# Cross attention laid out by hand over its groups, its scales on GpSimd, and the combine product behind the up products

## The reference

```python
x = x + tanh(g_xattn[0]) * L0_xattn(layernorm(x), ctx, ctx, Wq, bq, Wk, bk, Wv, bv, Wo, bo)
#   16 heads of 8; head h sees keys h, h+16, h+32, h+48 (4 of them); softmax; out @ Wo.T + bo
x = x + tanh(g_ffn[0]) * L0_ffn(layernorm(x), ...)
#   rmsnorm, self attention of 16 heads over 128 tokens, residual, rmsnorm,
#   8 experts of 256 (2 chosen a token) and a shared one, residual
x = x + tanh(g_xattn[1]) * L1_xattn(ctx, layernorm(x), w_sim, b_sim, W_qv, b_qv)
x = x + tanh(g_ffn[1]) * L1_ffn(layernorm(x), ...)
#   16 experts of 64 (2 chosen), a gated shared one
return x
```

## Time and profile before

| | us |
|---|---|
| three runs | 563.38 median (563.04 to 566.1) |
| profiled execution | 563.62, its span 561.9 |
| mean granted TensorE clock | 0.929 of 2.4 GHz |
| busy: PE, DVE, ScalarE, GpSimd | 467.4, 403.4, 265.8, 257.3 |
| start and cross attention | 0 to 67 |
| self attention | 67 to about 190 |
| router | about 190 to 218 |
| mixtures | 218 to 562 |

### The profile page before, as it was taken

One profiled execution on the slowest core, in us unless ns is written; L12 is line 12 of the kernel. 1 busy time (PEld: TensorE's weight loads), 2 busy tenths in 40 slices (PEclk: granted clock), 3 DMA queues, 4 the chain that ended last, 5 costly groups with the idle time before them and its releaser, 6 DMA issues.

```text
span 561.9 us, 10894 instructions
## 1 busy us (share of the span) xinstructions
PE 467.4 (83%) x3679; PEld 349.4 (62%) x3679; DVE 403.4 (72%) x1051; ACT 265.8 (47%) x494; POOL 257.3 (46%) x363
## 2 busy tenths in 40 slices
PE   2576279999999466999979988999798989798896
PEld 2344147676667354777757776768576766576674
DVE  6567568888987644895775677777877787677763
ACT  0211057777776234655536533644355346443452
POOL 6000079988960030555554544345445444343453
PEclk9878589999999855999989997999899999998999
DMA  6500000201010000200000000000000000000000
GB/s 163 173 0 0 0 3 2 85 23 51 3 34 19 1 0 0 48 0 1 1 2 0 2 1 2 1 0 0 0 0 1 0 1 1 20 0 21 0 20 19
DMA packets 19325, 9.79 MB, mean 17 GB/s; under 512 B 6508, under 2 KB 18765, under 8 KB 19277
## 3 DMA queue, kind: packets, MB, share of 16 engines
q1 hardware_dynamic: 16829, 8.77, 5.5%
q10 hardware_dynamic: 2448, 0.40, 0.4%
HBM read 8.12 MB, written 1.05 MB: 16 GB/s over the span
## 4 chain that ended last, share of the span: by engine, by line
PE 60%; DVE 18%; issue 8%; POOL 5%; ACT 5%; ACTq 2%; DVEq 1%; POOLq 0%
PE PS L1453 11%; PE PS L1455 10%; PE PS L1454 10%; DVE work L1062 3%; PE PS L1334 3%; PE PS L1323 3%; PE PS L1498 3%; PE PS L1328 2%; PE PS L1368 2%; PE PS L1301 2%; PE PS L1417 2%; PE PS L1239 1%; PE PS L1312 1%; DVE t_b L736 1%; POOL W0L_gate L421 1%
## 5 line engine op out<-in xcount | busy, mean ns | idle before, releaser
L461 POOL TENSOR_TENSOR HLO<-work,HHI 128x512 fp32r<-128x512 f32 x112 | 145.1, 1296 | 185.9 <-ACT HHI L625 185.4
L632 ACT ACTIVATE work<-PS 128x512 f32<-128x512 f32 x112 | 66.8, 597 | 110.1 <-PE PS L1455 106.3
L1062 DVE TENSOR_TENSOR work<-work,PS 128x512 f32<-128x512 f32 x104 | 71.0, 683 | 55.1 <-ACT work L632 53.5
L625 ACT ACTIVATE HHI<-work 128x512 fp32r<-128x512 f32 x111 | 69.5, 626 | 40.2 <-DVE work L1067 40.1
L1067 DVE TENSOR_TENSOR work<-PS,work 128x512 f32<-128x512 f32 x112 | 77.1, 691 | 12.1 <-PE PS L1455 3.4
L1498 PE MATMUL PS<-CWT,sel 128*128 128x512 bf16 (+1 forms) x68 | 27.2, 400 | 24.0 <-DVE work L1062 24.0
L870 DVE TENSOR_REDUCE nmax<-PS 128x4 f32<-128x512 f32 x64 | 42.2, 682 | 6.4 <-PE PS L1301 6.2
L531 ACT ACTIVATE EX<-PS 128x512 f32<-128x512 f32 x64 | 35.2, 605 | 13.3 <-PE PS L1312 13.2
L1453 PE MATMUL PS<-H2H,W0H_up 128*128 128x512 f32 (+1 forms) x72 | 36.8, 512 | 2.9 <-DVE work L1067 2.9
L1453 PE MATMUL PS<-H2H,W0H_gate 128*128 128x512 f32 (+1 forms) x72 | 32.7, 454 | 2.2 <-issue 1.5
L1498 PEld LDWEIGHTS PS<-CWT,sel 128*128 128x128 bf16 x68 | 6.6, 97 | 44.8 <-DVE work L1062 30.0
(11 more groups left out here) (290 smaller groups left out, 1174.7 us busy)
## 6 DMA issues: line engine op xcount, KB each, us to landing
X<-in_x_dram SPq DMA_DIRECT2D x4, 256.0 KB, 8.1
raw<-in_L_ffn_e_gate_dram SPq DMA_DIRECT2D x1, 1024.0 KB, 5.4
raw<-in_L_ffn_e_up_dram SPq DMA_DIRECT2D x1, 1024.0 KB, 7.7
out_dram<-X SPq DMA_DIRECT2D x4, 256.0 KB, 2.3
ctx_nat<-in_ctx_dram SPq DMA_DIRECT2D x1, 616.0 KB
raw<-in_L_ffn_We_gate_dram SPq DMA_DIRECT2D x1, 512.0 KB, 4.0
raw<-in_L_ffn_We_up_dram SPq DMA_DIRECT2D x1, 512.0 KB, 3.9
raw<-in_L_ffn_We_down_dram SPq DMA_DIRECT2D x1, 512.0 KB, 4.1
```

Source lines behind the costliest of these rows:

```text
L461: pool.tensor_tensor(HLO[t][:], HH[k % 2][:], HHI[t][:].bitcast(F32), ALU.subtract).then_inc(m_sem["lo"], 1)
L625: act.activation(HHI[turn_of(m, g, k)][:], HH[k % 2][:], ACT.Copy).then_inc(S["hi"], 1)
L632: act.activation(SG[c % 2][:], PS[:, c % 2, :], ACT.Silu).then_inc(S["silu"], 1)
L1062: dve.tensor_tensor(SG[c % 2][:], SG[c % 2][:], PS[:, 4, :], ALU.mult).then_inc(S["scaled"], 1)
```

## The change

- ScalarE issues ten DMAs instead of 17, the `smalls` move to SP's queue; the context comes in two halves. Only Wk, Wv, Wo are turned.
- The queries are not made: `fold_keys` multiplies the masked keys by Wq (untransposed), so that the turned tokens meet `KQ` directly; the query bias enters the scores as a product of `BQ` (bias broadcast) with the masked keys. `bo` is multiplied by the gate once (`tgbo`) and added to X by GpSimd (`bias_group`).
- All four groups are written out instead of a loop, with two buffers for most tiles, in an order by hand on each engine.
- GpSimd makes the scales of tokens 4 to 15 (`first_scales(1, G)`), all group normalisations (`normalised_group`), and the scales of self attention, one half of the batches at a time (`scales_of_half(0)` before the slots, `scales_of_half(1)` behind slot 0), with ALU.pow and one Newton step.
- The last group's probabilities, turns and `attend(3)` stand among the first slots of self attention on each engine.
- `keep_going`: 4 transposes of the identity before the slots, 6 behind the first slot and 6 behind the second.
- In `chunks` of PE the combine product (L1498) stands behind the up products.

`batches(slot, a, b)` now takes the slots' numbers themselves: `range(a, b)`. The diff, cut:

```diff
--- before.py
+++ after.py
...
+            tokens(0)
+            context(0)
+            context(1)
+            for g in range(1, G):
+                tokens(g)
...
+            def moments(at, n):
+
+                st = stats[:, at, :]
+                pool.tensor_tensor(p_a[:, 0:n], st[:, :, 1], st[:, :, 4], ALU.add)
+                pool.tensor_tensor(p_b[:, 0:n], st[:, :, 1], st[:, :, 4], ALU.subtract)
+                step(pool.tensor_tensor(p_c[:, 0:n], st[:, :, 2], st[:, :, 5], ALU.add))
+                pool.tensor_scalar(mean[:, at], p_a[:, 0:n], -0.5, None, ALU.mult)
+                pool.tensor_scalar(p_c[:, 0:n], p_c[:, 0:n], 1.0 / D, None, ALU.mult)
+                step(pool.tensor_tensor(p_b[:, 0:n], p_b[:, 0:n], p_b[:, 0:n], ALU.mult))
+                step(pool.tensor_scalar(p_b[:, 0:n], p_b[:, 0:n], 0.25, None, ALU.mult))
+                step(pool.tensor_tensor(var[:, at], p_b[:, 0:n], p_c[:, 0:n], ALU.add))
+
+            def inverse_root(y, v, t):
+
+                step(pool.tensor_tensor(y, v, less_half[:].broadcast_to([P, v.shape[1]]), ALU.pow))
+                step(pool.tensor_tensor(t, y, y, ALU.mult))
+                step(pool.tensor_tensor(t, t, v, ALU.mult))
+                step(pool.tensor_scalar(t, t, -0.5, 1.5, ALU.mult, ALU.add))
+                step(pool.tensor_tensor(y, y, t, ALU.mult))
...
+            def scales_of_half(k):
+                at = slice(k * HALF, (k + 1) * HALF)
+                pool.wait_ge(a_sem["st"], 2 * k + 2)
+                moments(at, HALF)
+                pool.tensor_scalar(var2[:, k, 0, :], var[:, at], LN_EPS, None, ALU.add)
+                step(pool.tensor_scalar(var2[:, k, 1, :], var[:, at], 1.0 + RMS_EPS, LN_EPS * RMS_EPS, ALU.mult, ALU.add))
+                inverse_root(rs2[:, k].rearrange("p a b -> p (a b)"), var2[:, k].rearrange("p a b -> p (a b)"), p_d[:])
+                pool.tensor_tensor(nmr[:, at], mean[:, at], rs2[:, k, 0, :], ALU.mult)
+                step(pool.tensor_tensor(p_a[:, 0:HALF], var2[:, k, 0, :], rs2[:, k, 0, :], ALU.mult))
+                step(pool.tensor_tensor(r2[:, at], p_a[:, 0:HALF], rs2[:, k, 1, :], ALU.mult))
...
+            def bias_group(g):
+                pool.wait_ge(a_sem["xn"], g + 1)
+                Xg = X[:, g * GB:(g + 1) * GB, :]
+                pool.tensor_tensor(Xg, Xg, tgbo[:].unsqueeze(1).broadcast_to([P, GB, D]), ALU.add).then_inc(a_sem["bias"], 1)
+
+            normalised_group(0)
+            pool.wait_ge(bias_in, 16 * 3)
+            pool.tensor_copy(BQ[:], bq_c[:].broadcast_to([P, P])).then_inc(a_sem["bq"], 1)
+            first_scales(1, G)
+            normalised_group(1)
+            pool.wait_ge(tg_ready, 1)
+            pool.wait_ge(bo_in, 16)
+            step(pool.tensor_scalar(tgbo[:], bo_r[:], tg[:, 0:1], None, ALU.mult))
+            bias_group(0)
+            bias_group(1)
+            for g in range(2, G):
+                normalised_group(g)
+                bias_group(g)
+            pool.memset(BB[:], 0.0)
...
-            batches(slot, 0, 3)
+            scales_of_half(0)
+            batches(slot, -3, 1)
+            scales_of_half(1)
+            batches(slot, 1, B)
...
+            folded_keys(0)
+            turned_group(0)
+            folded_values(0)
+            folded_keys(1)
+            folded_values(1)
+            exp_group(0)
+            turned_group(1)
+            folded_keys(2)
+            folded_values(2)
+            turned_probabilities(0)
+            exp_group(1)
+            turned_group(2)
+            folded_keys(3)
+            folded_values(3)
+            turned_probabilities(1)
+            exp_group(2)
+            turned_group(3)
...
+            turned_probabilities(2)
+            exp_group(3)
+            batches(slot, -4, -2)
+            turned_probabilities(3)
+            batches(slot, -2, B)
...
+            first_stats(0, 1)
+            first_scales(0, 1)
             first_stats(1, G)
-            dve.wait_ge(first_in, 16 * 6)
-            lnc(dve.tensor_scalar(bo_r[:], bo_r[:], 1.0 / H, None, ALU.mult))
-            dve.wait_ge(consts, 1)
-            queries_keys_values(0)
-            values_out(0)
+            masked_keys_values(0)
+            masked_keys_values(1)
+            less_row_maximum(0)
+            masked_keys_values(2)
+            probabilities(0)
+            less_row_maximum(1)
+            masked_keys_values(3)
             dve.wait_ge(tg_ready, 1)
-            with dve.Fori(0, G - 1) as g:
-                norm(g + 1)
-                less_row_maximum(g)
-                probabilities(g)
-                queries_keys_values(g + 1)
-                attended(g)
-                values_out(g + 1)
-            less_row_maximum(G - 1)
-            probabilities(G - 1)
-            attended(G - 1)
-            dve.wait_ge(a_sem["x"], G + 1)
-            moments()
-            lnc(dve.tensor_scalar(var2[:, 0:B], var[:], LN_EPS, None, ALU.add))
-            lnc(dve.tensor_scalar(var2[:, B:2 * B], var[:], 1.0 + RMS_EPS, LN_EPS * RMS_EPS, ALU.mult, ALU.add))
-            lnc(dve.tensor_scalar(rs2[:].bitcast(I32), var2[:].bitcast(I32), -0.5, RSQRT_SEED, ALU.mult, ALU.add))
-            for _ in range(3):
-                lnc(dve.scalar_tensor_tensor(out=t_d[:], in0=rs2[:], scalar=-0.5, in1=rs2[:], op0=ALU.mult, op1=ALU.mult))
-                lnc(dve.tensor_tensor(t_d[:], t_d[:], var2[:], ALU.mult))
-                lnc(dve.scalar_tensor_tensor(out=rs2[:], in0=t_d[:], scalar=1.5, in1=rs2[:], op0=ALU.add, op1=ALU.mult))
-            dve.scalar_tensor_tensor(out=nmr[:], in0=mean[:], scalar=-1.0, in1=rs2[:, 0:B], op0=ALU.mult, op1=ALU.mult).then_inc(b_sem["ln"], 1)
-            lnc(dve.tensor_tensor(t_d[:, 0:B], var2[:, 0:B], rs2[:, 0:B], ALU.mult))
-            lnc(dve.tensor_tensor(r2[:], t_d[:, 0:B], rs2[:, B:2 * B], ALU.mult))
-            dve.wait_ge(small_in, 16 * 7)
-            dve.tensor_scalar(tgb[:], bqv_r[:], tg[:, 1:2], None, ALU.mult)
+            attended(0)
+            probabilities(1)
+            less_row_maximum(2)
+            attended(1)
+            probabilities(2)
+            less_row_maximum(3)
+            attended(2)
...
+            queries_and_keys(0)
+            values_apart(0)
+            probabilities(3)
+            queries_and_keys(1)
+            values_apart(1)
+            turned_keys(0)
+            attended(3)
+            queries_and_keys(2)
+            batches(slot, -3, -1)
+            dve.wait_ge(small_in, 16 * 7)
+            dve.tensor_scalar(tgb[:], bqv_r[:], tg[:, 1:2], None, ALU.mult)
+            batches(slot, -1, B)
...
+            def keep_going(n, to):
+                for _ in range(n):
+                    pe.transpose(to, identf[:], identf[:])
...
+            def fold_keys(g):
+                pe.wait_ge(a_sem["kv_sb"], g + 1)
+                if g >= 1:
+                    pe.wait_ge(a_sem["v2_sb"], g)
+                pe.matmul(PS[:, 0, 0:GB * NK], w_nat[:, 3, :], KA4[g % 2], start=True, stop=True).then_inc(a_sem["kq"], 1)
...
+            keys_values(0)
+            fold_keys(0)
+            keys_values(1)
+            fold_values(0)
+            turn_group(0)
+            strided_scores(0)
+            fold_keys(1)
+            keys_values(2)
+            fold_values(1)
+            turn_group(1)
+            strided_scores(1)
+            fold_keys(2)
+            keys_values(3)
+            fold_values(2)
+            turn_probabilities(0)
+            attend(0)
+            turn_group(2)
+            fold_keys(3)
+            fold_values(3)
+            turn_probabilities(1)
+            strided_scores(2)
+            attend(1)
+            turn_group(3)
+            turn_probabilities(2)
+            strided_scores(3)
+            attend(2)
+            keep_going(4, PS[:, 4, 0:P])
...
-            batches(slot, 0, 6)
+            batches(slot, -6, -5)
+            pe.wait_ge(a_sem["xt"], G)
+            keep_going(6, PS[:, 7, 2 * P:3 * P])
+            batches(slot, -5, -4)
+            turn_probabilities(3)
+            keep_going(6, PS[:, 7, 2 * P:3 * P])
+            batches(slot, -4, -3)
+            attend(3)
+            batches(slot, -3, B)
...
                     split_product(c % 2, WH[m][0][:, c, :], WL[m][0][:, c, :], xh, xl).then_inc(S["g"], 1)
+                    if not (start and c < 2):
+                        pe.wait_ge(S["hid"], base + c)
+                    split_product(2 + c % 2, WH[m][1][:, c, :], WL[m][1][:, c, :], xh, xl).then_inc(S["u"], 1)
                     if first_of_expert(m, c):
                         e = c // per
                         pe.wait_ge(S["scaled"], g * NSC[m] + OFF[m][1] + e * per + 1)
                         pe.matmul(PS[:, 4, :], SEL[m][:, e, :], CWT[:, bass.ds(g * GT, GT)], start=True, stop=True).then_inc(S["bc"], 1)
-                    if not (start and c < 2):
-                        pe.wait_ge(S["hid"], base + c)
```

(1 more changed line is left out.)

325 lines of the change are left out of this document (176 added, 149 removed).

## The result

The changed kernel takes 544.95 us, the median of four executions (541.47 to 552.77), beside 563.23 us before. The ratio of the means is 0.9643, 95% interval 0.9556 to 0.9731. Run twice more, unchanged, it has 543.3 us (541.42 to 546.53, ratio 0.9629, interval 0.9594 to 0.9664) and 542.67 us (541.72 to 546.84, ratio 0.9634, interval 0.9597 to 0.967). The execution that was profiled with the result, 552.77 us, is the longest of its four, at a lower granted clock than the others, and the ratios, not the medians, leave out executions like it that are over 1.5% above the fastest of their kernel. So its lines stand here beside those of the first of the two repeats (e0_after), which was profiled at 543.07 us.

A forecast was written before the change was run, and what follows sets the result against it. Taken as bounds: cross attention with idle PE and low clock, GpSimd from 77.4 to 105.3 us, then PE, with `scaled` waits in the mixtures. From 563.6 us, -24.6 + 1.4 + 5.2 + 1 - 5 = -22.0 gave 541.6, range 532 to 554.

The forecast's parts named there:

- The front, -24.6: Cross attention up to `turn_input(0)`: overlapped groups bring it from 67.6 to 43 us, bounds -28.3 to -19.6.
- nearer to the high clock's 39.3: `turn_input(0)` taken at 43 us, between 39.3 at the high clock and 48 at 1.2 GHz.
- The power: GpSimd's `pow` in the scales: in no row, between 0 and 3 us, taken as 0.5.
- The first slots, +1.4: From `turn_input(0)` to GpSimd's end of slot 0: 15 us instead of 13.6, bounds +0.6 to +4.1.
- `scales_of_half(1)`, +5.2: Second half's scales on GpSimd behind slot 0: not hidden, 4.7 + 0.5 us, bounds 4 to 8.
- The dip, +1: PE may fall to 1.2 GHz in the gap at the second half's scales: +1 us, bounds 0 to 2.
- The mixtures, -5: `sel` product behind the up products shortens PE's waits for `scaled`: -5 us, bounds -2 to -8.
- 1 (the clock stays low, fillers without effect): Attention and first slots: clock stays at 1.2 GHz, idle transposes have no effect; 548.4 us, chance 0.17.
- 2 (a high clock all through, 534.6): Clock high all through and handovers as short as walked; 534.6 us, chance 0.12.
- 3 (the `sel` move only moves the wait): Mixtures: the moved `sel` product gains nothing, DVE ends these stretches; 546.6 us, chance 0.08.
- 4 (a dear power): GpSimd's `pow`, three times in a chain, eats the whole gain from 7.8 us each; 567.1 at 9, chance 0.04.
- 5 falls: Cross attention: DVE's fixed order holds each group back, `turn_input(0)` at 56; 554 us, chance 0.06.

The follow-up runs named there:

- e0_after: The first of two repeats of the changed kernel, unchanged; 543.3 us, profiled at 543.07 us.
- e2: The changed kernel with GpSimd's `pow` replaced by a line (1.5 - 0.5 v) in front of the Newton step; 541.83 us.
- e7: The changed kernel with GpSimd's `pow` done twice in each of its three places; 554.71 us.
- e5: The changed kernel with the second half's scales on GpSimd three slots later, after slot 3 instead of slot 0; 550.25 us.
- e3: The kernel before with one edit, the `sel` product moved behind the up products; 559.59 us beside 564.82.
- e4: The changed kernel with the `sel` product put back ahead of the second up product of a step; 552.63 us.
- e10: The changed kernel with the `sel` product one place further, also behind the down product of the chunk three back; 550.16 us.

## Why the prediction was right, and where not

The time, 541.6 us against 544.95, 543.3 and 542.67, is right, and so is its mechanism: groups overlapped (`turn_input(0)` twenty us sooner), scales in a chain on GpSimd, unchanged batches of 6.77 us, `sel` waits of 18.7 us for the 15 to 19 that I had named. That it is this close is in part luck: two terms were 3.3 and 2.3 us too hopeful, and in e0_after the clock of the mixtures gave 4.3 back that stand in no term. In the profile after, which had no such gift, the stages make -10.9 instead of -22.0.

1. **The front, -24.6, was -21.3** (e0_after; -17.5 in the profile after). The step that failed is the choice of 43 as "nearer to the high clock's 39.3". The line of one group was the right one to follow, but two pieces of it were too short. The statistics of the second group came at 37.9 us (41.8), not 33 to 33.6: +4.3. GpSimd then took 8.35 us to TensorE's turn instead of 5.7, the power being 2.93 for 0.5: +2.6. 39.3 + 4.3 + 2.6 = 46.2. Of the 4.3, about 2 are there by the first scores, whose products begin at 19.4 us and end at 21 where the walk had 17.5: it had 2.4 GHz from the start, and the clock rose at 18 (27 in the profile after). Another 1.5 are the first two `attend`, for which I took 0.7 us, the time of the kernel before, and which take 1.48 and 1.47 now. The rest, and how much of the 2 is the clock's, no run separates.
   The sum of 7.5 us a group for TensorE at 1.2 GHz was too small too: its 1.1 for the scores and 0.7 for `attend` are times at 2.4 GHz (the earlier trace rows and the row of 32.20 above), and at 1.2 the changed kernel takes 1.81 and 2.49. That is why TensorE is as late as GpSimd at the wait for Z, as e2 shows, which the walk didn't have.
2. **The power**, "near the small steps", was put at the wrong end of 0 to 3 us. It takes 2.30 us on 128x12 and 2.92 on 128x16, and with that one of the signs of being wrong that I had named, a `pow` of over 1 us, came true. The bound of 3 from seven 128x128 operations held. The small steps were well sized: beside the power they are seventeen, not eighteen, and take 7.47 - 2.92 = 4.55 us for the 4.7.
3. **The first slots, +1.4**: 14.98 against the 15 that I took; 16.1 in the profile after, where the clock is low, within the bounds.
4. **`scales_of_half(1)`, +5.2, was 7.5**, in full on the path, as e2 and e7 show (2.8 less, 2.9 more). That it "isn't hidden" was right even for a later place, where e5 shows it to cost 10.7.
5. **The dip, +1, was +0.5.**
6. **The mixtures, -5, were -8.7 in e0_after and -4.4 in the profile after.** The waits went as worked out, 5.3 us less, and TensorE's idle time there fell by 4.4 and 4.9 us (35.0 to 30.6 and 30.1). The other 4.3 us of e0_after are busy time (308.9 to 304.6), with the lost clock down from 11.5 to 5.5 us. What I left out is that a wait of 2.5 to 3.2 us is at times followed by a fall of the clock and at times not, by a pattern that isn't tied to the moved product.

Together in e0_after: -21.3 + 1.4 + 7.5 + 0.5 - 8.7 = -20.6, the 561.9 to 541.3 of the spans.

Of the signs of being right, two didn't come. Products at half clock are not gone between 45 and 60 us: the granted clock is 0.50 from 44.8 to 47.7 and 0.58 from 51.4 to 55 in e0_after. GpSimd's first `sel` memset is at 71.99, not 63, the front being 3.2 us later, the power dearer, and more of slot 1 ahead of it than I had counted.

Of the rivals, 1 (the clock stays low, fillers without effect) was half right: in the profile of after the clock is 0.50 from 43.5 to 61 us, and its time, 552.77, is beyond the rival's 548.4. But it belongs to some executions and not to the kernel, and the idle turns did not decide it: with or without them the mixtures start at 206 us. 2 (a high clock all through, 534.6) came in no execution. 3 (the `sel` move only moves the wait) falls by e3 and e4; it comes near to what e10 does. 4 (a dear power) had the right mechanism at a little over a third of its break-even, and in two places of the three: the first is off the path. 5 falls: `turn_input(0)` at 46 to 50, not 56.

## What to carry to other kernels

Price an operation that no row shows at the far end of its bounds before it goes into a chain, and ask of each chain link which engine is only just behind: removing 2.9 us of GpSimd gave 0.5 where TensorE was as late, and 2.8 where it wasn't. A block of one engine's work is best put where the pipeline is still filling; in the steady stage, where GpSimd was busy for 17.5 of 20 us, the same 7.5 us cost 10.7. Moving a product behind others ahead of a wait paid once (4.0 to 4.5 us), and the next step of the same kind cost more than it gave, since VectorE waited for that product. Take the price of a product at the clock that it will run at, and look whether its order or its banks change with the edit: `attend` was put at half of its time or less.

## What the runs showed that I had not expected

- GpSimd's `pow` takes 2.27 to 2.30 us on 128x12 and 2.90 to 2.93 us on 128x16, against 0.20 to 0.24 for its other operations of that size: 4 elements more of each partition cost 0.63 us, so, if the cost is a fixed part and one by the element, it is 0.16 us for each and some 0.4 us beside.
- The granted clock after the same 2.87 us wait of TensorE at the same point of the program was 1.00 in one execution and 0.66 in another, also of one and the same kernel. The frequent pattern repeats on two chips. Between two patterns lie 5.5 us of lost clock over the mixtures and 4.3 us of their length, as much as the `sel` move is worth.
- The clock's first rise came near 18 us or near 27 in otherwise equal starts, and moved the first turn of Z by 3.9 us.
- An `attend` of the same eight 64x128 products takes 1.48 us at 2.4 GHz and 2.49 at 1.2, where the kernel before took 0.72 and 1.22 with another order and other banks. What giving it back its order would save, no run shows.
- 128x128 float32 products of the identity take two instructions each, its transposes one, each with a median of 0.42 us at this place.
